# Graph 0 of a two-layer graph network: where W1's parts are made, in which order the inputs are loaded, and when the degree sums run

## The reference, cut to what matters

```python
# layer 0: hypergraph convolution, twice (W1 then W2), per graph
H  = (adj != 0);  w = adj[0, :]                      # the first row weighs the columns
Dn = 1 / (H @ w)                                     # the degree sum of each node
Be = 1 / H.sum(axis=0)
conv(x, W, b) = Dn * (H @ (Be * (H.T @ (x @ W.T)))) + b
h = layer_norm(relu(conv(x, W1, b1))) * gamma + beta
x = layernorm(x + conv(h, W2, b2) + x)
# layer 1
agg = (adj @ x) / max(adj.sum(-1), 1e-6)
x = layernorm(x + relu(concat([x, agg]) @ WL.T))
```

## Time and profile before

| | |
|---|---|
| median of 3 runs | 1089.95 us (1089.07 to 1090.24) |
| the profiled execution's own time | 1090.12 us |
| its span | 1088.5 us |
| TensorE busy (matmul) | 1073.5 us, 99% |
| VectorE, ScalarE, GpSimd busy | 746.4, 372.7, 217.5 us |
| TensorE busy in 0 to 50 us | 41.17 us |
| VectorE busy in 0 to 50 us | 38.59 us |
| granted clock | 1.00 in every slice, 0.999 in the mean |

### The profile page before, as it was taken

How to read it: one execution, slowest core, us unless ns; L and a number is a source line. 1 busy time by engine, 2 the same in 40 slices (tenths; PEclk the granted TensorE clock), 3 DMA queues, 4 the chain that set the end, 5 groups by cost and what they waited for, 6 DMA issues and landing times.

```text
span 1088.5 us, 18849 instructions
## 1 busy us (share of the span) xinstructions
PE 1073.5 (99%) x6235; PEld 919.3 (84%) x6235; DVE 746.4 (69%) x1972; ACT 372.7 (34%) x811; POOL 217.5 (20%) x276
## 2 busy tenths in 40 slices
PE   7899999999999999999999999999999999999997
PEld 7789698896988969898798978989789896888966
DVE  6875596665965768758687486774867747867326
ACT  5372213622145321453115431154302533026230
POOL 1623004220041202312032120411204120041000
PEclk9999999999999999999999999999999999999999
DMA  8207712076210662125611355115542065300001
GB/s 295 59 1 156 155 42 57 0 154 155 57 40 24 130 157 55 39 54 121 143 48 39 83 126 117 41 39 112 128 87 68 9 142 127 68 11 1 1 1 39
DMA packets 63871, 86.44 MB, mean 79 GB/s; under 512 B 8164, under 2 KB 53864, under 8 KB 63848
## 3 DMA queue, kind: packets, MB, share of 16 engines
q1 hardware_dynamic: 63376, 85.75, 34.4%
q10 hardware_dynamic: 472, 0.40, 0.1%
HBM read 77.73 MB, written 8.39 MB: 79 GB/s over the span
## 4 chain that ended last, share of the span: by engine, by line
PE 91%; DVE 6%; DMA 1%; issue 1%; ACT 0%; SPq 0%; DVEq 0%
PE bank L882 41%; PE bank L993 10%; PE bank L1056 10%; PE bank L975 10%; PE bank L912 8%; PE bank L1023 3%; PE bank L1028 3%; PE bank L1029 3%; PE bank L1001 3%; PE bank L1041 1%; DMA raw<-in_adj_dram 1%; DVE adjT L666 1%; DVE unread L618 1%; DVE HT L671 1%; DVE m_lo L653 1%
## 5 line engine op out<-in xcount | busy, mean ns | idle before, releaser
L882 PE MATMUL bank<-yv,adjT 128*128 128x257 f32 x1024 | 223.3, 379 | 0.0
L882 PEld LDWEIGHTS bank<-yv,adjT 128*128 128x128 f32 x1024 | 193.6, 189 | 31.8 <-issue 3.8
L469 ACT ACTIVATE small<-mv,small 128x1 f32<-128x1 f32 x192 | 56.6, 295 | 348.8 <-DVE mv L648 248.8
L403 POOL TENSOR_TENSOR xres<-x_in 128x256 f32<-128x256 f32 x64 | 45.6, 748 | 410.3 <-DMA out_dram<-xres 406.8
L882 PE MATMUL bank<-x_hi,H 128*128 128x256 f32 x512 | 126.0, 287 | 0.0
L912 PE MATMUL bank<-x_hi,H 128*128 128x258 f32 x512 | 123.8, 289 | 1.9 <-DVE x_lo L702 1.4
L882 PE MATMUL bank<-x_lo,H 128*128 128x256 f32 x512 | 122.4, 280 | 0.0
L993 PE MATMUL bank<-gW2T,xnT 128*128 128x256 f32 x512 | 122.1, 381 | 0.0
L882 PE MATMUL bank<-m_hi,HT 128*128 128x256 f32 x512 | 121.6, 280 | 0.0
L882 PE MATMUL bank<-m_lo,HT 128*128 128x256 f32 x512 | 120.9, 279 | 0.0
L912 PE MATMUL bank<-x_lo,H 128*128 128x256 f32 x512 | 119.3, 282 | 0.1
(11 more groups left out here) (102 smaller groups left out, 1814.4 us busy)
## 6 DMA issues: line engine op xcount, KB each, us to landing
raw<-in_adj_dram SPq DMA_DIRECT2D x112, 256.0 KB, 8.6
adjB<-in_adj_dram SPq DMA_DIRECT2D x224, 128.0 KB, 3.4
x_in<-in_x_dram SPq DMA_DIRECT2D x31, 256.0 KB, 4.6
out_dram<-xres SPq DMA_DIRECT2D x108, 64.0 KB, 1.6
raw<-in_adj_dram SPq DMA_DIRECT2D x8, 512.0 KB, 10.4
w_row<-in_adj_dram SPq DMA_DIRECT2D x8, 512.0 KB, 3.7
out_dram<-xres SPq DMA_DIRECT2D x4, 256.0 KB, 2.2
W1n<-in_L_gnn_W_dram SPq DMA_DIRECT2D x1, 512.0 KB, 11.0
```

Of the source, the lines that this page charges most:

```text
L403: nc.gpsimd.tensor_tensor(xres[:, t, :], x_in[:, t, :], x_in[:, t, :], ALU.add).then_inc(xb_part, 1)
L469: nc.scalar.activation(std[:, i:i + 1], mv[:, which, i, 1:2], ACT.Sqrt, bias=eps_c)\
L882: last = mm(bank(stage, i)[:, 0:n_cols], lhsT, rhs, start=(k == 0 and part == 0), stop=(k == NT - 1 and part == parts - 1))
```

## The change: what it does

- **Loads.** The rows of adj go earlier in SP's queue: rows 1 is issued ahead of the second pair of x, w behind rows 4, W1 behind rows 6, W2 and beta behind rows 7, and WL behind beta.
- **TensorE.** W1 is transposed in step 5 of the walk, W2 in step 6, WL in step 7, and bW2 after five of the eight c of e = 6 (before: after four).
- **W1's parts.** ScalarE makes `W1_high` straight from the PSUM bank; VectorE makes `W1_low` from the bank and `W1_high` in step 6, and this empties the bank; VectorE makes `W1_cross` by one instruction each behind the degree sums. The SBUF copy `W1T`, ScalarE's two scalings by 4096 and GpSimd's four subtractions go.
- **Residual.** GpSimd's residual of graph 0 waits for 1/Dn (`rDn_ready` at 2) in place of the last HT tile.
- **VectorE.** Degree sum 0 stands in step 5, sum 1 behind the walk ahead of `sum_bW2`, and sums 2 to 7 behind the last `m_lo` of S1. 1/Be of the first six tiles is made by two instructions over six columns, once all six are full; the eight banks are one PSUM tensor for this.

```diff
@@ -38,6 +38,7 @@
 DN_LAG = 3
+FIRST_DN = 2
@@ -62,7 +63,7 @@
-    BETWEEN = {1: ("gamma",), 3: ("W1", "W1"), 5: ("WL", "WL"), NT - 1: ("W2", "W2")}
+    BETWEEN = {1: ("gamma",), NT - 3: ("W1", "W1"), NT - 2: ("W2", "W2"), NT - 1: ("WL", "WL")}
     N_SIDE = TRANSPOSE_BANKS[0]
@@ -144,7 +145,7 @@
         x_in, _, _ = place("x_in", [P, NT, D], F32)
-        xres, xres_at, _ = place("xres", [P, NT, D], F32)
+        xres, _, _ = place("xres", [P, NT, D], F32)
         w_row, _, _ = place("w_row", [P, C], F32)
@@ -180,7 +181,6 @@
         gamma_n, _, _ = place("gamma_n", [P, P], F32, nxt)
-        W1T, _, _ = place("W1T", [P, ND, DH], F32, xres_at)
@@ -192,7 +192,8 @@
-        banks = [ctx.enter_context(nc.psum_tensor(f"bank{n}", [P, 512], F32)) for n in range(N_BANKS)]
+        psum = ctx.enter_context(nc.psum_tensor("bank", [P, N_BANKS, 512], F32))
+        banks = [psum[:, n, :] for n in range(N_BANKS)]
@@ -219,8 +220,7 @@
             sem(n) for n in ("z_high_done", "z_high_scaled", "z_cross_done", "shift_done"))
-        W1_high_done, W1_low_done, W1_low_scaled, W1_cross_done = (
-            sem(n) for n in ("W1_high_done", "W1_low_done", "W1_low_scaled", "W1_cross_done"))
+        W1_high_done, W1_cross_done = sem("W1_high_done"), sem("W1_cross_done")
         deg_done, rdeg_done, o_done, sum_done = (sem(n) for n in ("deg_done", "rdeg_done", "o_done", "sum_done"))
@@ -314,21 +314,21 @@
             load_first_rows(0)
+            load_first_rows(1)
             load_first_x(1)
-            load_first_rows(1)
             load_first_rows(2)
+            load_first_rows(3)
+            load_first_x(2)
+            load_first_rows(4)
             load_w(0)
-            load_first_x(2)
-            load_first_rows(3)
+            load_first_rows(5)
+            load_first_x(3)
+            load_first_rows(6)
             sp.dma_start(W1n[:, :, :], W1.rearrange("(t p) d -> p t d", p=P)).then_inc(W1_loaded, 16)
-            load_first_rows(4)
-            load_first_x(3)
-            load_first_rows(5)
-            sp.dma_start(WLn[:, :, :], WL.rearrange("(t p) d -> p t d", p=P)).then_inc(WL_loaded, 16)
-            load_first_rows(6)
             load_first_rows(7)
...
             sp.dma_start(beta_row[:, :], beta.partition_broadcast(P)).then_inc(beta_loaded, 16)
+            sp.dma_start(WLn[:, :, :], WL.rearrange("(t p) d -> p t d", p=P)).then_inc(WL_loaded, 16)
             sp.dma_start(b1_row[:, :], b1.partition_broadcast(P)).then_inc(bias_loaded, 16)
@@ -383,19 +383,10 @@
-            for d in range(ND):
-                pool.wait_ge(W1_high_done, d + 1)
-                nc.gpsimd.tensor_tensor(W1_low[:, d, :], W1T[:, d, :], W1_high[:, d, :].bitcast(F32), ALU.subtract)\
-                  .then_inc(W1_low_done, 1)
-            for d in range(ND):
-                pool.wait_ge(W1_low_scaled, d + 1)
-                nc.gpsimd.tensor_tensor(W1_cross[:, d, :], W1_high[:, d, :].bitcast(F32),
-                                        W1_cross[:, d, :].bitcast(F32), ALU.subtract).then_inc(W1_cross_done, 1)
             for j in range(NT // 2):
...
             pool.wait_ge(bias_loaded, 16 * 2)
-            pool.wait_ge(W1_low_done, ND)
-            pool.wait_ge(HT_ready, NT)
+            pool.wait_ge(rDn_ready, 2)
@@ -477,7 +468,9 @@
                 if name == "W1":
-                    take_weight("W1", part, W1T[:, part, :])
+                    act.wait_ge(*set_full("W1", part))
+                    nc.scalar.activation(W1_high[:, part, :], set_bank("W1", part)[:, :], ACT.Copy, scale=ROUND_DOWN)\
+                      .then_inc(W1_high_done, 1)
                 elif name == "WL":
@@ -497,16 +490,6 @@
                     take_set(BETWEEN[c][1], 1)
-                if c == 4:
-                    for d in range(ND):
-                        act.wait_ge(*set_empty("W1", d))
-                        nc.scalar.activation(W1_high[:, d, :], W1T[:, d, :], ACT.Copy, scale=ROUND_DOWN)\
-                          .then_inc(W1_high_done, 1)
-                if c == NT - 2:
-                    for d in range(ND):
-                        act.wait_ge(W1_low_done, d + 1)
-                        nc.scalar.activation(W1_cross[:, d, :], W1_low[:, d, :].bitcast(F32), ACT.Copy, scale=SPLIT)\
-                          .then_inc(W1_low_scaled, 1)
             for e in range(NT):
@@ -677,7 +660,7 @@
                 dve.wait_ge(beta_loaded, 16)
-                dve.wait_ge(dn_ready, 5)
+                dve.wait_ge(dn_ready, FIRST_DN)
                 for o in range(ND):
@@ -697,6 +680,25 @@
+            def take_first_rBe():
+                for e in range(N_SIDE):
+                    dve.wait_ge(*full("S1", e, 0))
+                nc.vector.tensor_scalar(be_safe[:, 0:N_SIDE], psum[:, 0:N_SIDE, D:D + 1].rearrange("p e c -> p (e c)"),
+                                        1.0, None, ALU.max).then_inc(be_done, N_SIDE)
+                dve.wait_ge(be_done, N_SIDE)
+                nc.vector.reciprocal(rBe[:, 0:N_SIDE], be_safe[:, 0:N_SIDE]).then_inc(rBe_ready, N_SIDE)
+            def take_W1_low(d):
+                dve.wait_ge(W1_high_done, d + 1)
+                nc.vector.tensor_tensor(W1_low[:, d, :], set_bank("W1", d)[:, :], W1_high[:, d, :].bitcast(F32),
+                                        ALU.subtract).then_inc(bank_empty[set_of["W1", d][0]], 1)
+            def take_W1_cross(d):
+                dve.wait_ge(*set_empty("W1", d))
+                nc.vector.scalar_tensor_tensor(out=W1_cross[:, d, :], in0=W1_low[:, d, :].bitcast(F32), scalar=-SPLIT,
+                                               in1=W1_high[:, d, :].bitcast(F32), op0=ALU.mult, op1=ALU.add)\
+                  .then_inc(W1_cross_done, 1)
             def split_first_x_lo(tiles):
@@ -709,20 +711,28 @@
                     build_HT_columns(c - 2)
-                if c >= 3:
-                    sum_Dn(c - 3, 0, unread, (first_rows_loaded[c - 3], 16))
-                if c == NT - 1:
-                    sum_bW2()
+                if c == NT - 3:
+                    sum_Dn(0, 0, unread, (first_rows_loaded[0], 16))
+                if c == NT - 2:
+                    take_W1_low(0)
+                    take_W1_low(1)
+            for t in range(1, FIRST_DN):
+                sum_Dn(t, 0, unread, (first_rows_loaded[t], 16))
+            sum_bW2()
+            take_first_rBe()
+            take_m_lo("S1", 0, 0, 0)
             build_HT_columns(NT - 2)
-            take_rBe(0, 0)
-            take_rBe(1, 0)
+            take_m_lo("S1", 1, 0, 1)
             build_HT_columns(NT - 1)
-            for e in range(NT):
+            for e in range(2, N_SIDE):
                 take_m_lo("S1", e, 0, e)
-                if e + 2 < NT:
-                    take_rBe(e + 2, 0)
-                if N_SIDE - 3 <= e < N_SIDE:
-                    sum_Dn(e + NT - N_SIDE, 0, unread, (first_rows_loaded[e + NT - N_SIDE], 16))
+            for e in range(N_SIDE, NT):
+                take_rBe(e, 0)
+                take_m_lo("S1", e, 0, e)
+            for t in range(FIRST_DN, NT):
+                sum_Dn(t, 0, unread, (first_rows_loaded[t], 16))
+            take_W1_cross(0)
+            take_W1_cross(1)
             build_rDn(0)
@@ -959,7 +969,7 @@
                 for c in range(NT):
-                    if e == N_SIDE and c == NT // 2:
+                    if e == N_SIDE and c == NT - 3:
                         transpose_set("bW2", 0)
...
             pe.wait_ge(W2T_scaled, NH // 2)

```

## The result

The changed kernel takes 1093.51 us (median of 8, 1093.24 to 1093.97), the kernel before 1089.77 in the same runs: a ratio of 1.0035 with an interval of 1.0024 to 1.0046. It is **slower by 3.7 us**. I had forecast 1090.3 with a range up to 1092.6, so the measured time lies outside the range, 0.9 above its upper end. The profiled spans are 1091.7 and 1088.5, 3.2 apart.

The account below looks back on a forecast made before the run. TensorE's queue from the first M product on was taken as the bound. -0.5 (M0) + 0.1 (GpSimd wait) + 0.7 (clock) = +0.3 on the profiled 1090.1 gave 1090.4, as a median 1090.3; range 1088.3 to 1092.6.

Parts of the forecast that it names:

- The walk: Steps up to S1's end: with rows early and weight sets late, S1 ends at 32.9, 4.2 us sooner.
- The tail on VectorE: VectorE behind the last m_lo: put-off sums, W1_cross, 1/Dn, z_low and z_cross leave M0 only 0.5 us sooner.
- M0: Start of the first M product on TensorE, at 49.78 us before the change, forecast at 49.3.
- The gap in TensorE: TensorE idle from 44.2 to 49.3, ahead of M0: possible half pace afterwards, taken as 0.7 us, bounds 0 and 2.8.
- GpSimd's second z_cross: GpSimd's second half of z_cross, wanted by M of node tile 4: 0.1 us of wait.
- (b): From M0 to node tile 4: half pace for 2.8 us plus two other delays, +3.9, 1093.9; chance 0.16.
- Its other two terms: Behind the half pace in (b): both z_cross wait for whole additions, +0.9; GpSimd's halves 0.7 late.
- My signs of being wrong: TensorE's wait under 3 us; M0 over 1.5 from 49.3; W1 set before 19; S1's end outside 32 to 34.

Follow-up runs that it names:

- the kernel with M0 at 45.55: The changed kernel with the residual behind z_cross and degree sums 1 to 5 and both W1_cross in VectorE's waits: 1087.07 us (0.9979).

## Why the prediction was wrong, point by point

- **The walk: right.** S1's end was put at 32.9 (measured 33.1), 1/Be of the first six at 28.9 (29.4). The first W1 set came at 19.07, inside the bound but 0.8 earlier than WL's old slot says; from there to e = 6 (about 29.0) it took 9.9 us for a forecast 8.9, which took it back. The bank hand-offs to VectorE are 0.3 to 0.5 of that (0.7 in place of 0.2 to 0.4); the rest I did not trace.
- **The tail on VectorE: the mechanism right, sized short.** M0 was put at 49.3 and came at 50.3. The last m_lo was 0.5 late (36.8 for 36.3). Six sums were taken 1.24 apart; they are 1.34 apart (36.75, 38.09), because in the program each waits for the one before to have put out its sum, and the row at 15.00 had no sum behind it. From the first to W1_cross they take 7.84 (36.75 to 44.59) for 7.45: +0.4. The two z_cross lost 0.87 where I had 0.7. W1_cross, 1/Dn and z_low came within 0.15 each of what I had, and cancel; together the 1.0. That GpSimd's additions cause the loss in z_cross is shown (1.28 without them, 2.15 beside them). By the rule of the Trainium skill (SBUF — State Buffer, "SBUF: two separate sides") each z_cross could wait for a whole addition, 0.7; they lost 0.43 each, each W1_cross in one run 0.52. The trace stays within the rule, below its worst case.
- **The gap in TensorE: this step failed.** "I take the middle, 0.7", between 0 and 2.8. It was 2.45. The wait fell across a real drop of the granted clock, and the half pace lasted 5.3 us of work, not the start's 2.8. The start was a poor row for it: its granted clock reads 1.00 while the products are 0.22 apart, so I had the cost of the state at hand but not how long it lasts. A middle between "nothing" and "all" is not a mechanism; with the wait of 5 us that my own sum gave, the row nearest to it was the one behind 4.2 us of nothing, and the rule of the Trainium skill stood beside it. Even "the whole", 1.4, would have been 1.05 short, since the half pace lasted nearly twice as long as at the start. The range held half pace for 5 us at its upper end; it was the 1.0 at M0 that carried the time past it.
- **GpSimd's second z_cross: no wait** (0.1 forecast); behind the half pace its work was not wanted before it was done. The mark I used for it was a little late: M of node tile 4 stands 11.9 us behind M0 in the kernel before (61.72), not 12.2.
- **The rival that came true is (b)**, at 0.16: half pace for about twice the start's time. Its figure with the half pace alone, 1092.3, is 1.2 below what came, and 1.0 of that is M0. Its other two terms did not come: z_cross lost 0.2 more than forecast, not 0.9, and GpSimd's halves cost nothing. With M0 at 50.3 and 2.45 for the clock the sum is 1090.1 + 2.97 = 1093.1, against 1093.4 of the profiled execution. My signs of being wrong (a wait under 3 us, M0 more than 1.5 off) did not come either, because none was set on how long a half pace lasts.
- **The parts** were never weighed apart in the prediction, and there lay what was to be found. By the medians: loads alone -2.4; W1 on VectorE alone +0.8, not clear of noise and with a fall of the clock in it; putting the sums back -2.65; residual later -1.2. The first two are against the kernel before, the last two against the changed one. They don't add up to the whole, since the clock's 2.45 hangs on the sum of them; how the loss divides among the parts stays open.

Open: the last 0.2 us of the span, what sets the moment of the fall (2.5 to 4.4 us behind the last product in six traces) and whether it comes at all behind a wait of 2.2 us, and 0.5 us by which the kernel with M0 at 45.55 ends later than M0 and its one wait account for.

## What to carry to other kernels

Work put off from a full engine still has to be done ahead of the same instruction: put it into that engine's own waits (here 1.4, 2.0 and three times 0.6 us), and count, from the last input to the first output, what stands in a row. A gain that ends in one long wait of TensorE can be worse than the several short waits that it replaced, because the clock falls in it; check the longest wait and not only the sum. When a change has several parts, price each alone: here one part alone made the kernel 2.4 us faster, and all together made it 3.7 us slower.

## What the runs showed of the hardware

- TensorE waits of 1.0 to 1.8 us left the pace alone. Of two waits of 2.2 us one did too, and behind the other the granted clock fell to 0.50 for 3.3 us, 0.7 us after work began again. Waits of 3.9, 4.4, 4.9, 5.8 and 8.6 us brought the granted clock to 0.50 in the profiled execution, 2.5 to 4.4 us behind the last product, and it stayed for 4.2 to 6.0 us after work began again (50.3 to 55.7 in the changed kernel). From M0 to node tile 3 this cost 1.9 to 2.7 us (10.24 to 11.06 for 8.38).
- VectorE and GpSimd in each other's way, by form: two SBUF operands of 512 columns 0.64 each alone and 1.08 to 1.17 beside additions; a sum of 1024 columns 1.22 to 1.57; an operation with one PSUM operand (z_low, m_lo) nothing. H and HT, with one SBUF operand, went from 0.69 to 1.76 beside GpSimd's subtractions for W1. The loss beside additions is much the same for a long and a short instruction, so short ones pay most for their length: 1/Dn's first instruction 0.17 to 0.69. GpSimd's additions took 0.58 to 0.70 each in the stretch behind M0 and 1.54 beside a row of sums.
